# The D term of a state space mixer: products with diagonal matrices on TensorE against a product on VectorE and an add on GpSimd

## The chip, the cores and the metric

The kernel runs on one core of one Trainium2 chip. Its time is the device time of one execution in microseconds (us), taken as the median of three runs. The engines are TensorE (PE in the rows, with its weight loads as PEld), VectorE (DVE), ScalarE (ACT), GpSimd (POOL) and the DMA queues. Each engine works through its own instructions in order; they meet at semaphores.

## The reference, cut to what matters

The model has two layers, and the first begins with a mixer of the Mamba-2 kind over 8 sequences of 512 tokens and 128 features. The scan over time carries a state of 4 heads x 64 x 128; the kernel computes it in chunks of 128 tokens. The D term is the last summand of the line that computes y:

```
xs = silu(conv(x @ in_proj_w.T)[..., :256] + conv_b)        # 256 inner channels, 4 heads of 64
h  = h * dA_t + einsum('bh,bhp,bn->bhpn', dt_t, x_t, B_t)   # for each token
y  = einsum('bhpn,bn->bhp', h, C_t)
y  = ys + D[None, None, :, None] * xs                       # the D term
y  = y * silu(z)
y  = y * rsqrt(mean(y * y) + EPS) * norm_w
out = y @ out_proj_w.T
```

Behind the mixer come a layer of 8 experts, an attention layer and a second layer of experts. The change doesn't touch them.

## The kernel before, in words

The function `mixer` writes one program for each engine. All five step through the same slots s; slot s belongs to sequence b = s // 4 and has the place c = s % 4 in it. In this document "slot c2" is a slot with c = 2. A slot takes up chunk s (128 tokens of 128 partitions), and finishes earlier ones: the product that gives y for chunk t = s - 1, the output projection of chunk s - 2, the norm of chunk s - 3, the logits of chunk s - 4. In the same slot the next sequence (f = b + 1) has a quarter of its convolution computed, and the one after it gets its normalisation. The order within a slot is written out by hand; there is no planner. Sequence 7 has no next one, so in its slots there is no convolution, and from sequence 5 on there are no statistics for a later one.

TensorE in one slot, in order: in slot c3 first a transpose of `da48` (L662), which waits for VectorE's last copy out of bank 7 in the slot before (`o_r`, L569); the transposes of xs and the product B x C of chunk s (L668, L669); the spread of the decays (L675); the transposes of yz, B and xn2 into bank 6 (L683, L685, L689), the first of which waits for yz of chunk s - 2; half of the convolution (three matmuls for each tap, L630 to L632); for chunk t the product with the carried state (L724), then for each half i of the 256 channels one product of the chunk with the diagonal matrix `diag_d[:, i]` (L729) and two products of `mt` with `xdt` that add to the same bank (L732); the new state (L742); the other half of the convolution; the output projection (L755) and the logits (L758).

VectorE in one slot, in order: xdt (L487), the scan that spreads the decays `lt` (L493), y1 = carried part x decay (L499; c = 0 of a sequence has none), mt (L502), in slot c3 the four steps for the next sequence's decays (L507 to L516, the last is da_bd), xn2 (L523; it waits for `rs2` of GpSimd), y2 = y1 + bank 5 (L530), the new state (L535 or, for the first chunk, L538), yz = y2 x silu(z) (L544; for the first chunk L548, straight from the bank), then x (L565; it waits for the output projection), statistics and routing; in slot c2 also ve1 (L586) and h_lo (L610), in slot c3 at its very beginning nm1 (L474).

GpSimd in one slot, in order: state_d = state x decay (L258; chunks with t % 4 of 1 or 2, so slots c2 and c3), in slot c3 the weights wo_g (L265), rs2 (L270, a power of one column), rr (L275, a power of one column, which waits for ScalarE's ysq of this slot), one of the three steps of the residual (L282, L285, L288, in slots c1, c2, c3), and in slot c2 rs1 (L295).

ScalarE evicts the convolution (xc, L397), z (zs, L318) and the transposes, and in slot c1 changes its function table four times; `da` (L388) there waits for VectorE's dax (L598).

At the start GpSimd builds `diag_d` from the identity and the D values, in the loop's slot -7.

Of the kernel before, what the change touches and what calls it, by code (L numbers as in the profile page):

```python
# [10 lines left out]
P = 128  # L11
# [4 lines left out]
ALU = mybir.AluOpType  # L16
# [3 lines left out]
NB = 8  # L20
# [4 lines left out]
DI = 256  # L25
# [82 lines left out]
def mixer(nc, k, a):  # L108
# [5 lines left out]
    with ExitStack() as ctx:  # L114
        def sb(name, shape, dt=F32):
# [2 lines left out]
        wc_hi = sb("wc_hi", [P, NTAP, SEQ], F32R); wc_lo = sb("wc_lo", [P, NTAP, SEQ], F32R)  # L118
        wz = sb("wz", [P, DI + NH]); wz_hi = sb("wz_hi", [P, DI + NH], F32R); wz_lo = sb("wz_lo", [P, DI + NH], F32R)
        conv_b = sb("conv_b", [P, 4]); dt_b = sb("dt_b", [P, NH]); a_log = sb("a_log", [P, NC * NH]); a_exp = sb("a_exp", [P, NC * NH])  # L120
        d_bc = sb("d_bc", [P, DI]); diag_d = sb("diag_d", [P, 2, P]); norm_w = sb("norm_w", [P, 2])
        wo = sb("wo", [P, 2, D]); wo_g = sb("s_wo_g", [P, 2, 2, D]); gw = sb("gw", [P, NE])
        ident4 = sb("ident4", [P, NC * P]); pick = sb("pick", [48, 16]); csel_f = sb("csel_f", [48, NC]); csel = sb("csel", [48, NC], F32R); head = sb("head", [48, NH]); zero16 = sb("zero16", [16, P])
        cT = sb("cT", [P, 2 * NB]); cu = sb("cu", [P, 2 * NB])
# [22 lines left out]

        k.sems((
            "c_in", "c_in1", "x_in0", "x_in1", "x_in2", "w_in0", "w_in1", "w_in2", "aw_in", "pad_in", "r_out") + tuple(f"rows_in{b}" for b in range(NB)) + (
            "set_pool", "set_diag", "set_pick", "c_cu", "c_mm", "c_mod", "c_row_mm", "c_row", "c_gate", "c_rk", "w_mul", "w_hi", "w_lo",  # L150
            "f_mm", "f_ev", "l1_st", "l1_ag", "l1_ve", "l1_rs", "l1_nm", "l1_xn", "h_lo", "res_1", "res_2", "res_x", "s_wog",
            "d_raw", "d_neg", "d_exp", "d_ln", "d_dt", "d_dax", "d_da", "d_hi", "d_t", "d_bd", "o_w", "o_r",
            "s_xmm", "s_lmm", "s_amm", "s_aev", "s_xdt", "s_lt", "s_mt", "s_xdw", "s_ymm", "s_smm", "s_y1", "s_y2", "s_yz", "s_state", "s_sd",
            "s_ss", "s_rr", "o_x", "l2_st", "l2_ag", "l2_ve", "l2_rs", "l2_xn", "r_mx", "r_mi"))
        block = ctx.enter_context(nc.Block())

# [73 lines left out]
        def _(pool):  # L230
# [12 lines left out]
            def body(s, b, c):  # L243
                if s == -7:
                    pool.wait_ge(S["w_in2"], 16 * 6)
                    for i in range(2):
                        ins = g_.tensor_scalar(wo[:, i, :], wo[:, i, :], norm_w[:, i:i + 1], None, ALU.mult)
                    ins.then_inc(S["set_pool"], 1)
                    for i in range(2):
                        ins = g_.tensor_tensor(diag_d[:, i, :], ident[:], d_bc[:, i * P:i * P + P], ALU.mult)  # L250
                    ins.then_inc(S["set_diag"], 1)
                t = s - 1
                if chunk(t) and t % NC in (1, 2):
                    wait(pool, "s_state", n_y(t))
                    wait(pool, "o_r", seventh["cum", t // NC] + 1)
                    wait(pool, "s_state", n_y(t))
                    at = (t % NC) * NH
                    g_.tensor_tensor(hv(state_d[:]), hv(state[:]), bc3(ctot[:, (t // NC) % 2, 1, at:at + NH], NH, HD), ALU.mult).then_inc(S["s_sd"], 1)  # L258
                if b + 1 < NB and c == 3 and b >= -1:
                    f = b + 1  # L260
                    pool.wait_ge(S[f"rows_in{f}"], 16)
                    pool.wait_ge(S["set_pool"], 2)
                    if f >= 2:
                        wait(pool, "o_w", seventh["out", NC * (f - 1) + 1] + 1)
                    g_.tensor_tensor(wo_g[:, f % 2], wo[:], over_rows(rows[:, f, GA0, :], 2), ALU.mult).then_inc(S["s_wog"], 1)  # L265
                t = s - 3
                if chunk(t):
                    wait(pool, "l2_ve", t + 1)
                    wait(pool, "l2_xn", t - 1)
                    g_.tensor_tensor(rs2[:, t % 2, :], ve2[:], half_neg[:, 0:1], ALU.pow).then_inc(S["l2_rs"], 1)  # L270
                t = s - 1
                if chunk(t):
                    wait(pool, "s_ss", t + 1)
                    wait(pool, "o_x", t - 1)
                    g_.tensor_tensor(rr[:, t % 2, :], ss[:, t % 2, :], half_neg[:, 0:1], ALU.pow).then_inc(S["s_rr"], 1)  # L275
                if b >= -1 and b + 1 < NB and c > 0:
                    f = b + 1
                    wait(pool, "l1_xn", f + 1)
                    if c == 1:
                        pool.wait_ge(S[f"rows_in{f}"], 16)  # L280
                        wait(pool, "res_x", f)
                        g_.tensor_tensor(rt[:], xn1[:, f % 2], over_rows(rows[:, f, RES_G, :], NC), ALU.mult).then_inc(S["res_1"], 1)  # L282
                    elif c == 2:
                        wait(pool, "res_1", f + 1)
                        g_.tensor_tensor(rt[:], rt[:], over_rows(rows[:, f, RES_B, :], NC), ALU.add).then_inc(S["res_2"], 1)  # L285
                    else:
                        wait(pool, "res_2", f + 1)
                        g_.tensor_tensor(x[:, f * NC:f * NC + NC, :], x[:, f * NC:f * NC + NC, :], rt[:], ALU.add).then_inc(S["res_x"], 1)  # L288

                g = b + 3  # L290
                if g < NB and c == 2:
                    wait(pool, "l1_ve", g + 1)
                    wait(pool, "l1_nm", g)
                    wait(pool, "l1_xn", g)
                    g_.tensor_tensor(rs1[:], ve1[:], half_neg[:], ALU.pow).then_inc(S["l1_rs"], 1)  # L295
# [121 lines left out]
        def _(dve):  # L417
# [8 lines left out]
            def body(s, b, c):  # L426
# [54 lines left out]
                if chunk(s):  # L481
                    q = b % 2
                    wait(dve, "s_xmm", s + 1)
                    wait(dve, "s_ymm", s - 1)
                    wait(dve, "s_xdw", NH * n_y(s - 1))
                    wait(dve, "d_dt", b + 1)
                    v.tensor_tensor(hv(xdt[:, s % 2, :]), hv(bank[2][:, 0:DI]), bc3(dt[:, q, c * NH:c * NH + NH], NH, HD), ALU.mult).then_inc(S["s_xdt"], 1)  # L487
                if front and c == 1:
                    wait(dve, "d_raw", f + 1)
                    v.scalar_tensor_tensor(out=dtn[:], in0=dtw[:], scalar=-1.0, in1=dtw[:], op0=ALU.mult, op1=ALU.min).then_inc(S["d_neg"], 1)  # L490
# [3 lines left out]
                t = s - 1  # L494
                if chunk(t) and t % NC:
                    wait(dve, "s_ymm", t + 1)
                    wait(dve, "s_y2", n_y(t) - 1)
                    at = (t % NC) * NH
                    v.tensor_tensor(hv(y1[:]), hv(bank[5][:, DI:2 * DI]), bc3(ctot[:, (t // NC) % 2, 0, at:at + NH], NH, HD), ALU.mult).then_inc(S["s_y1"], 1)  # L499
                if chunk(s):  # L500
# [23 lines left out]
                t = s - 1  # L524
                if chunk(t):
                    tb, tc = t // NC, t % NC
                    if tc:
                        wait(dve, "s_y1", n_y(t))
                        wait(dve, "s_yz", t)
                        v.tensor_tensor(y2[:], y1[:], bank[5][:, 0:DI], ALU.add).then_inc(S["s_y2"], 1)  # L530
                    if tc < 3:
                        wait(dve, "s_smm", n_y(t) + 1)
                        if tc:
# [5 lines left out]
                    if t >= 2:  # L539
                        wait(dve, "s_amm", turned[t] + 1)  # L540
                        wait(dve, "s_ss", t - 1)
                    if tc:
                        wait(dve, "s_y2", n_y(t))
                        v.tensor_tensor(yz[:, t % 2, 0:DI], y2[:], zs[:, tb % 2, tc, :], ALU.mult).then_inc(S["s_yz"], 1)  # L544
                    else:
                        wait(dve, "s_ymm", t + 1)
                        wait(dve, "f_ev", ring["z", tb, 3] + 1)
                        v.tensor_tensor(yz[:, t % 2, 0:DI], bank[5][:, 0:DI], zs[:, tb % 2, tc, :], ALU.mult).then_inc(S["s_yz"], 1)  # L548
                if gl < NB and c == 2:
                    wait(dve, "x_in0" if gl == 0 else "x_in1" if gl == 1 else "x_in2", 16)  # L550
                    wait(dve, "l1_ag", NC * gl)
# [68 lines left out]
        def _(pe):  # L620
# [31 lines left out]
            def body(s, b, c):  # L652
# [64 lines left out]
                if chunk(t):  # L717
# [5 lines left out]
                        wait(pe, "s_state", n_y(t))  # L723
                        t_.matmul(bank[5][:, DI:2 * DI], xc[:, tb % 2, 3, tcols], state[:], start=True, stop=True)  # L724
                    if t == 0:
                        pe.wait_ge(S["set_diag"], 1)
                        wait(pe, "c_row", 4)
                    for i in range(2):
                        t_.matmul(bank[5][:, i * P:i * P + P], xc[:, tb % 2, i, tcols], diag_d[:, i, :], start=True, stop=True)  # L729
                        wait(pe, "s_mt", t + 1)  # L730
                        for h in (2 * i, 2 * i + 1):
                            mm = t_.matmul(bank[5][:, h * HD:h * HD + HD], mt[:, t % 2, h * P:h * P + P], xdt[:, t % 2, h * HD:h * HD + HD],  # L732
                                           start=False, stop=True, skip_group_check=True)
                    mm.then_inc(S["s_ymm"], 1)
                    if front and c == 0:
                        z(f, 2)
# [24 lines left out]
            slots(body)  # L761

    k.retired = [(n, NT) for n in (
        "s_xmm", "s_lmm", "s_xdt", "s_lt", "s_mt", "s_ymm", "s_yz", "s_ss", "s_rr", "o_x", "l2_st", "l2_ag", "l2_ve", "l2_rs", "l2_xn", "r_mx", "r_mi",
        "l1_st", "l1_ag")] + [(n, 3 * NB) for n in ("s_smm", "s_y1", "s_y2", "s_state")] + [("s_sd", 2 * NB), ("s_xdw", 3 * NB * NH)] + [(n, NB) for n in (
        "l1_ve", "l1_rs", "l1_nm", "l1_xn", "h_lo", "res_1", "res_2", "res_x", "s_wog", "d_raw", "d_neg", "d_exp", "d_ln", "d_dt", "d_dax", "d_da",
        "d_hi", "d_t", "d_bd")] + [("f_mm", len(ring)), ("f_ev", len(ring)), ("o_w", len(seventh)), ("o_r", len(seventh)), ("s_amm", len(turned)), ("s_aev", len(turned))]

# [917 lines left out]
```

## Time and profile before

| | |
|---|---|
| median of 3 runs | 729.47 us (727.29 to 730.06) |
| profiled execution, own time | 731.17 us |
| its span | 727.9 us |
| mean granted TensorE clock | 0.91 |
| PE busy | 583.6 us (80%) |
| PEld busy | 480.0 us (66%) |
| DVE busy | 427.3 us (59%) |
| ACT busy | 348.9 us (48%) |
| POOL busy | 282.1 us (39%) |

The span runs from the first to the last instruction; the execution's own time is 3.3 us longer. The mixer's loop over chunks takes from about 41 us to about 312 us of the span, the rest belongs to the later layers. Busy shares are means over stages that are bound by different things, so the rows that count for this change are those of the mixer's loop. In a timeline a row can stand for several instructions of one line (x2, x4), and TensorE's instructions overlap, so what one of them takes of the engine is read from start to start.

### The profile page before, as it was taken

What the parts mean: (1) busy time and instruction counts of PE and PEld (TensorE: products, weight loads), DVE (VectorE), ACT (ScalarE), POOL (GpSimd) and SP (SyncE); (2) the same over time, 40 slices, a digit from 0 to 9 for tenths busy, and PEclk for the clock granted to TensorE, in tenths of its full rate; (3) what the DMA queues carried; (4) which work ended last, traced back from release to release, by engine and by line L of the source; (5) the groups of instructions that cost most, each with busy time, mean ns of one, the idle gap of its engine ahead of it and who ended that gap; (6) DMA issues with size and microseconds to landing.
All of it is one profiled execution on the core that took longest, in us unless ns stands there. A gap on an engine that the chain in (4) does not pass through costs nothing.

```text
span 727.9 us, 13867 instructions
## 1 busy us (share of the span) xinstructions
PE 583.6 (80%) x3569; PEld 480.0 (66%) x3569; DVE 427.3 (59%) x1583; ACT 348.9 (48%) x947; POOL 282.1 (39%) x339
## 2 busy tenths in 40 slices
PE   5698989999998998727687787867519999999694
PEld 3577777777777877614465565555519999999631
DVE  4437675758586657843554645355526666666447
ACT  4654748373747453325444434332105666665424
POOL 3303141414232331311104533444545667676423
PEclk9889999999999998958999989899659999999977
DMA  8599999900000000026000000000112222222193
GB/s 272 196 180 176 180 173 179 137 2 1 1 2 1 2 0 1 1 78 193 0 1 24 30 13 19 31 31 30 34 50 60 69 73 67 72 67 73 52 234 101
DMA packets 74846, 52.91 MB, mean 73 GB/s; under 512 B 10392, under 2 KB 68760, under 8 KB 74512
## 3 DMA queue, kind: packets, MB, share of 16 engines
q1 hardware_dynamic: 69200, 41.30, 28.8%
q0 software_dynamic: 4320, 8.99, 3.7%
q10 hardware_dynamic: 1248, 1.71, 0.6%
q8 instruction: 34, 0.56, 0.3%
q14 instruction: 44, 0.36, 0.2%
HBM read 40.88 MB, written 29.48 MB: 97 GB/s over the span
## 4 chain that ended last, share of the span: by engine, by line
PE 37%; DVE 7%; issue 5%; ACT 3%; POOL 1%; DMA 1%; SPq 0%; ACTq 0%; DVEq 0%; POOLq 0%
PE bank L1575 9%; PE bank L1593 9%; PE bank L1492 6%; PE bank L1477 4%; DVE work L1311 1%; PE bank L1468 1%; PE bank L1458 1%; DVE nmx L1294 1%; POOL queue L1066 1%; PE bank L1566 1%; PE bank L1462 1%; ACT work L1166 1%; DVE st_f L1409 1%; ACT h_all L1161 1%; PE bank L1521 1%
## 5 line engine op out<-in xcount | busy, mean ns | idle before, releaser
L1098 POOL DMA_INDIRECT results<-yw,xg x71 | 75.7, 1066 | 56.4 <-ACT yw L1188 51.6
L275 POOL TENSOR_TENSOR rr<-ss,half_neg 128x1 f32<-128x1 f32 x32 | 17.6, 550 | 190.3 <-ACT ysq L403 190.3
L1575 PE MATMUL bank<-xt,wc 128*128 128x128 f32 x568 | 78.0, 281 | 1.2 <-issue 0.7
L1492 PE MATMUL bank<-vv,work 128*128 128x128 f32 x256 | 41.1, 309 | 44.7 <-ACT work L1166 30.0
L1593 PE MATMUL bank<-w,ht 128*128 x568 | 75.8, 277 | 0.1
L1575 PEld LDWEIGHTS bank<-xt,wc 128*128 128x128 f32 x568 | 70.6, 196 | 3.9 <-issue 3.1
L630 PE MATMUL bank<-h_hi,wc_hi 128*128 128x512 f32 x128 | 59.4, 464 | 13.2 <-ACT xc L397 12.2
L1593 PEld LDWEIGHTS bank<-w,ht 128*128 128x128 f32 x568 | 69.7, 193 | 0.3 <-issue 0.3
L1066 POOL DMA_INDIRECT queue<-row,pos x64 | 62.7, 980 | 18.1 <-issue 17.5
L1492 PEld LDWEIGHTS bank<-vv,work 128*128 128x128 f32 x256 | 34.4, 209 | 52.2 <-ACT work L1166 33.5
L1382 DVE COPY wc<-w 128x516 f32 x71 | 36.2, 511 | 37.6 <-PE bank L1575 33.9
L1155 ACT ACTIVATE work<-bank,nmx 128x512 f32<-128x512 f32 x32 | 22.0, 687 | 66.1 <-DVE nmx L1294 66.1
L631 PE MATMUL bank<-h_hi,wc_lo 128*128 128x512 f32 x128 | 52.5, 410 | 0.0
L632 PE MATMUL bank<-h_lo,wc_hi 128*128 128x512 f32 x128 | 52.4, 409 | 0.0
L1395 DVE TENSOR_SCALAR ht<-bank,wc 128x128 f32<-128x128 f32 x142 | 42.8, 342 | 14.0 <-PE bank L1575 13.5
L397 ACT ACTIVATE xc<-bank,conv_b 128x512 f32<-128x512 f32 x32 | 22.0, 687 | 59.4 <-PE bank L632 59.3
L1182 ACT ACTIVATE xt<-bank 128x128 f32<-128x128 f32 x71 | 19.7, 278 | 62.9 <-PE bank L1566 62.4
L1203 ACT ACTIVATE ht<-bank,wc 128x128 f32<-128x128 f32 x142 | 43.2, 353 | 1.4 <-PE bank L1575 1.3
L1075 POOL TENSOR_TENSOR rs_a<-ve_a,half_neg 128x4 f32<-128x4 f32 x8 | 8.2, 1026 | 84.1 <-DVE ve_a L1241 83.1
L630 PEld LDWEIGHTS bank<-h_hi,wc_hi 128*128 128x128 f32 x128 | 25.3, 198 | 21.0 <-ACT xc L397 13.8
L493 DVE TENSOR_TENSOR_SCAN lt<-bank,ident 128x512 f32<-128x512 f32 x32 | 38.8, 1213 | 0.1
L732 PE MATMUL bank<-xdt,mt 128*128 128x64 f32 x256 | 36.5, 266 | 0.0
(276 smaller groups left out, 1491.6 us busy)
## 6 DMA issues: line engine op xcount, KB each, us to landing
queue<-in_pad_rows SPq DMA_DIRECT2D x8, 2178.0 KB, 33.0
xg<-queue SPq DMA_DIRECT2D x71, 66.0 KB, 1.8
w<-in_w SPq DMA_DIRECT2D x2, 2048.0 KB, 10.6
rows<-mod_rows SPq DMA_DIRECT2D x8, 384.0 KB, 5.9
h_all<-results SPq DMA_DIRECT2D x8, 256.0 KB, 4.8
work<-results SPq DMA_DIRECT2D x8, 256.0 KB, 5.4
out_x<-x SPq DMA_DIRECT2D x8, 256.0 KB, 2.3
results<-yw,xg POOLq DMA_INDIRECT x71, 2.4
```

Source lines behind the costliest of these rows:

```text
L493: v.tensor_tensor_scan(lt[:, s % 2, :], bank[3][:], ident4[:], 0.0, ALU.mult, ALU.add).then_inc(S["s_lt"], 1)
L630: t_.matmul(dst, l_hi, r_hi, start=first, stop=False)
L631: t_.matmul(dst, l_lo, r_hi, start=False, stop=False)
L632: return t_.matmul(dst, l_hi, r_lo, start=False, stop=last)
L732: mm = t_.matmul(bank[5][:, h * HD:h * HD + HD], mt[:, t % 2, h * P:h * P + P], xdt[:, t % 2, h * HD:h * HD + HD], start=False, stop=True, ...
L1066: pool.indirect_dma_start(k.queue, bass.IndirectOffsetOnAxis(ap=pos[:, s, i, c:c + 1], axis=0), row[:, s * NC + c, i, :], None).then_inc(S ...
L1098: pool.indirect_dma_start(k.results, bass.IndirectOffsetOnAxis(ap=xg[:, c, D:D + 1].bitcast(I32), axis=0), yw[:, c, :], None).then_inc(S[f ...
L1203: ac.activation(ht[:, p, g * P:g * P + P], bank[2 + p][:, g * P:g * P + P], ACT.Relu, bias=wc[:, p, FF + g:FF + g + 1]).then_inc(S["ht_a"], 1)
L1395: v.tensor_scalar(ht[:, p, g * P:g * P + P], bank[6 + p][:, g * P:g * P + P], wc[:, p, FF + g:FF + g + 1], 0.0, ALU.add, ALU.max).then_inc ...
L1492: mm = t_.matmul(bank[4 if n % 2 else 0][:, 0:D], pt[:, n % 3, i * P:i * P + P], vv[:, s % 2, i, :], start=(i == 0), stop=(i == NC - 1))
L1575: mm = t_.matmul(bank[(2 if g < NG // 2 else 6) + p][:, g * P:g * P + P], wc[:, p, g * P:g * P + P], xt[:, p, :], start=True, stop=True)
L1593: mm = t_.matmul(bank[4 + p][:, 0:D], ht[:, p, g * P:g * P + P], w2[:, e, g, :], start=(g == 0), stop=(g == NG - 1))
```

## The change

The diagonal matrices go. VectorE multiplies the transposed chunk (bank 2) with the D values into a new tile `xd`, right behind xdt. GpSimd adds y1 and xd into a new tile `yx`, as its first step of the slot; VectorE's y2 is then yx plus bank 5. For the first chunk of a sequence, which has no y1, y2 is xd plus bank 5, an instruction that was not there before, and yz always reads y2.

```
-        d_bc = sb("d_bc", [P, DI]); diag_d = sb("diag_d", [P, 2, P]); norm_w = sb("norm_w", [P, 2])
+        d_bc = sb("d_bc", [P, DI]); xd = sb("xd", [P, 2, DI]); yx = sb("yx", [P, DI]); norm_w = sb("norm_w", [P, 2])
...
 @block.gpsimd
-                    for i in range(2):
-                        ins = g_.tensor_tensor(diag_d[:, i, :], ident[:], d_bc[:, i * P:i * P + P], ALU.mult)
-                    ins.then_inc(S["set_diag"], 1)
                 t = s - 1
+                if chunk(t) and t % NC:
+                    wait(pool, "s_y1", n_y(t))
+                    wait(pool, "s_xd", t + 1)
+                    wait(pool, "s_y2", t)
+                    g_.tensor_tensor(yx[:], y1[:], xd[:, t % 2, :], ALU.add).then_inc(S["s_yx"], 1)
                 if chunk(t) and t % NC in (1, 2):
                     wait(pool, "s_state", n_y(t))
...
 @block.vector (behind xdt)
+                if chunk(s):
+                    if s == 0:
+                        dve.wait_ge(S["w_in2"], 16 * 6)
+                    wait(dve, "s_y2", s - 1)
+                    v.tensor_tensor(xd[:, s % 2, :], bank[2][:, 0:DI], d_bc[:], ALU.mult).then_inc(S["s_xd"], 1)
...
                 if chunk(t) and t % NC:
                     wait(dve, "s_ymm", t + 1)
-                    wait(dve, "s_y2", n_y(t) - 1)
+                    wait(dve, "s_yx", n_y(t) - 1)
...
                 if chunk(t):
                     tb, tc = t // NC, t % NC
+                    wait(dve, "s_yz", t)
                     if tc:
-                        wait(dve, "s_y1", n_y(t))
-                        wait(dve, "s_yz", t)
-                        v.tensor_tensor(y2[:], y1[:], bank[5][:, 0:DI], ALU.add).then_inc(S["s_y2"], 1)
+                        wait(dve, "s_yx", n_y(t))
+                    else:
+                        wait(dve, "s_ymm", t + 1)
+                    v.tensor_tensor(y2[:], yx[:] if tc else xd[:, t % 2, :], bank[5][:, 0:DI], ALU.add).then_inc(S["s_y2"], 1)
...
-                    if tc:
-                        wait(dve, "s_y2", n_y(t))
-                        v.tensor_tensor(yz[:, t % 2, 0:DI], y2[:], zs[:, tb % 2, tc, :], ALU.mult).then_inc(S["s_yz"], 1)
-                    else:
-                        wait(dve, "s_ymm", t + 1)
-                        wait(dve, "f_ev", ring["z", tb, 3] + 1)
-                        v.tensor_tensor(yz[:, t % 2, 0:DI], bank[5][:, 0:DI], zs[:, tb % 2, tc, :], ALU.mult).then_inc(S["s_yz"], 1)
+                    wait(dve, "s_y2", t + 1)
+                    wait(dve, "f_ev", ring["z", tb, 3] + 1)
+                    v.tensor_tensor(yz[:, t % 2, 0:DI], y2[:], zs[:, tb % 2, tc, :], ALU.mult).then_inc(S["s_yz"], 1)
...
 @block.tensor
-                    for i in range(2):
-                        t_.matmul(bank[5][:, i * P:i * P + P], xc[:, tb % 2, i, tcols], diag_d[:, i, :], start=True, stop=True)
-                        wait(pe, "s_mt", t + 1)
-                        for h in (2 * i, 2 * i + 1):
-                            mm = t_.matmul(bank[5][:, h * HD:h * HD + HD], mt[:, t % 2, h * P:h * P + P], xdt[:, t % 2, h * HD:h * HD + HD],
-                                           start=False, stop=True, skip_group_check=True)
+                    wait(pe, "s_mt", t + 1)
+                    for h in range(NH):
+                        mm = t_.matmul(bank[5][:, h * HD:h * HD + HD], mt[:, t % 2, h * P:h * P + P], xdt[:, t % 2, h * HD:h * HD + HD], start=True, stop=True)
                     mm.then_inc(S["s_ymm"], 1)
```

## Rows read from the trace of the kernel before

**Rows 1.** Busy time by stretch: length, then each engine's busy us, TensorE's clock, DMA share, GB/s
```profile
140.00:180.00 40.00, 36.49 (x225) 30.37 (x224) 29.22 (x99) 24.56 (x70) 13.15 (x18) 1.00 0.02 4
126.10:129.50 3.40, 3.40 (x12) 2.75 (x11) 0.00 (x0) 2.90 (x9) 2.78 (x4) 0.53 1.25 154
...
283.10:289.90 6.80, 6.70 (x28) 6.04 (x29) 3.77 (x13) 2.33 (x9) 1.10 (x2) 0.51 0.00 1
```

**Rows 2.** One line's instructions: min/median/max ns, first and last start, shapes
```profile
L729 PE MATMUL bank<-diag_d,xc x128: 271/275/527, 51.9 to 302.9; 128*128 128x128 f32 x128
...
L487 DVE TENSOR_TENSOR xdt<-bank,dt x32: 403/424/426, 42.0 to 297.5; 128x256 f32<-128x256 f32 x32
```

**Rows 3.** Who waited for whom, 50 to 310 us: us in total, times, longest
```profile
DVE y L499 <- PE bank L732: 43.0, 22, 5.5
DVE x L565 <- PE bank L758: 23.7, 15, 2.3
...
ACT da L388 <- DVE dax L598: 5.4, 6, 1.1
```

**Rows 4.** Timeline of TensorE, slots c2 and c3 of sequence 3: start, us
```profile
163.05 0.38 PE L729 MATMUL bank<-diag_d,xc 128*128 128x128 f32 x2
163.27 0.56 PE L732 MATMUL bank<-xdt,mt 128*128 128x64 f32 x4
163.66 0.44 PE L729 MATMUL bank<-diag_d,xc 128*128 128x128 f32 x2
163.94 0.56 PE L732 MATMUL bank<-xdt,mt 128*128 128x64 f32 x4
...
167.97 0.29 PE L662 MATMUL bank<-ident,da 128*48 128x128 f32 x1 [1.02 <-DVE lg L569]
...
176.86 0.41 PE L683 MATMUL bank<-ident,yz 128*128 128x128 f32 x2 [0.39 <-DVE yz L544]
```

**Rows 5.** Timeline of VectorE over the same two slots
```profile
164.53 0.42 DVE L499 TENSOR_TENSOR y<-bank,ctot 128x256 f32<-128x256 f32 x1 [3.89 <-PE bank L732]
...
165.47 0.34 DVE L523 TENSOR_SCALAR xn<-x,mv,rs 128x128 f32<-128x128 f32 x1
...
168.29 1.08 DVE L586 TENSOR_SCALAR ve<-mv 128x4 f32<-128x4 f32 x1
...
170.52 0.57 DVE L474 SCALAR_TENSOR_TENSOR nm<-mv,rs 128x4 f32<-128x4 f32 x1
...
172.77 0.42 DVE L499 TENSOR_TENSOR y<-bank,ctot 128x256 f32<-128x256 f32 x1 [0.22 <-PE bank L732]
...
174.65 0.68 DVE L516 TENSOR_TENSOR da_bd<-da,head 48x512 fp32r<-48x512 f32 x1
175.26 0.33 DVE L523 TENSOR_SCALAR xn<-x,mv,rs 128x128 f32<-128x128 f32 x1
```

**Rows 6.** Timeline of GpSimd over the same two slots
```profile
168.09 1.27 POOL L285 TENSOR_TENSOR rt<-rt,rows 128x512 f32<-128x512 f32 x1
...
170.45 0.62 POOL L258 TENSOR_TENSOR state_d<-state,ctot 128x256 f32<-128x256 f32 x1
171.02 0.73 POOL L265 TENSOR_TENSOR s_wo_g<-wo,rows 128x256 f32<-128x256 f32 x1
171.71 0.54 POOL L270 TENSOR_TENSOR rs<-ve,half_neg 128x1 f32<-128x1 f32 x1
```

**Rows 7.** Timeline of GpSimd, slot c2 of sequence 5
```profile
235.96 1.75 POOL L285 TENSOR_TENSOR rt<-rt,rows 128x512 f32<-128x512 f32 x1
```

**Rows 8.** Timeline of VectorE, slot c2 of sequence 6
```profile
265.72 0.35 DVE L523 TENSOR_SCALAR xn<-x,mv,rs 128x128 f32<-128x128 f32 x1 [0.97 <-POOL rs L270]
```

**Rows 9.** Timeline of TensorE: the beginning of slot c2's convolution, sequences 2 and 3
```profile
125.59 0.57 PE L630 MATMUL bank<-h_hi,wc_hi 128*128 128x512 f32 x1 [1.39 <-ACT xc L397]
...
161.12 0.50 PE L630 MATMUL bank<-h_hi,wc_hi 128*128 128x512 f32 x1 [1.38 <-ACT xc L397]
```

**Rows 10.** Timeline of VectorE, the last three y1, of sequence 7
```profile
294.15 0.42 DVE L499 TENSOR_TENSOR y<-bank,ctot 128x256 f32<-128x256 f32 x1 [0.41 <-PE bank L732]
...
298.97 0.40 DVE L499 TENSOR_TENSOR y<-bank,ctot 128x256 f32<-128x256 f32 x1
...
303.63 0.42 DVE L499 TENSOR_TENSOR y<-bank,ctot 128x256 f32<-128x256 f32 x1 [1.28 <-PE bank L732]
```

More of the change, by code:

```diff
@@ L149, in mixer @@
             "c_in", "c_in1", "x_in0", "x_in1", "x_in2", "w_in0", "w_in1", "w_in2", "aw_in", "pad_in", "r_out") + tuple(f"rows_in{b}" for b in range(NB)) + (
-            "set_pool", "set_diag", "set_pick", "c_cu", "c_mm", "c_mod", "c_row_mm", "c_row", "c_gate", "c_rk", "w_mul", "w_hi", "w_lo",
+            "set_pool", "set_pick", "c_cu", "c_mm", "c_mod", "c_row_mm", "c_row", "c_gate", "c_rk", "w_mul", "w_hi", "w_lo",
             "f_mm", "f_ev", "l1_st", "l1_ag", "l1_ve", "l1_rs", "l1_nm", "l1_xn", "h_lo", "res_1", "res_2", "res_x", "s_wog",
             "d_raw", "d_neg", "d_exp", "d_ln", "d_dt", "d_dax", "d_da", "d_hi", "d_t", "d_bd", "o_w", "o_r",
-            "s_xmm", "s_lmm", "s_amm", "s_aev", "s_xdt", "s_lt", "s_mt", "s_xdw", "s_ymm", "s_smm", "s_y1", "s_y2", "s_yz", "s_state", "s_sd",
+            "s_xmm", "s_lmm", "s_amm", "s_aev", "s_xdt", "s_lt", "s_mt", "s_xdw", "s_ymm", "s_smm", "s_y1", "s_xd", "s_yx", "s_y2", "s_yz", "s_state", "s_sd",
             "s_ss", "s_rr", "o_x", "l2_st", "l2_ag", "l2_ve", "l2_rs", "l2_xn", "r_mx", "r_mi"))
@@ L725, in body @@
                     if t == 0:
-                        pe.wait_ge(S["set_diag"], 1)
                         wait(pe, "c_row", 4)
-                    for i in range(2):
-                        t_.matmul(bank[5][:, i * P:i * P + P], xc[:, tb % 2, i, tcols], diag_d[:, i, :], start=True, stop=True)
-                        wait(pe, "s_mt", t + 1)
-                        for h in (2 * i, 2 * i + 1):
-                            mm = t_.matmul(bank[5][:, h * HD:h * HD + HD], mt[:, t % 2, h * P:h * P + P], xdt[:, t % 2, h * HD:h * HD + HD],
-                                           start=False, stop=True, skip_group_check=True)
+                    wait(pe, "s_mt", t + 1)
+                    for h in range(NH):
+                        mm = t_.matmul(bank[5][:, h * HD:h * HD + HD], mt[:, t % 2, h * P:h * P + P], xdt[:, t % 2, h * HD:h * HD + HD], start=True, stop=True)
                     mm.then_inc(S["s_ymm"], 1)
@@ L763, in mixer @@
     k.retired = [(n, NT) for n in (
-        "s_xmm", "s_lmm", "s_xdt", "s_lt", "s_mt", "s_ymm", "s_yz", "s_ss", "s_rr", "o_x", "l2_st", "l2_ag", "l2_ve", "l2_rs", "l2_xn", "r_mx", "r_mi",
-        "l1_st", "l1_ag")] + [(n, 3 * NB) for n in ("s_smm", "s_y1", "s_y2", "s_state")] + [("s_sd", 2 * NB), ("s_xdw", 3 * NB * NH)] + [(n, NB) for n in (
+        "s_xmm", "s_lmm", "s_xdt", "s_lt", "s_mt", "s_ymm", "s_xd", "s_y2", "s_yz", "s_ss", "s_rr", "o_x", "l2_st", "l2_ag", "l2_ve", "l2_rs", "l2_xn", "r_mx", "r_mi",
+        "l1_st", "l1_ag")] + [(n, 3 * NB) for n in ("s_smm", "s_y1", "s_yx", "s_state")] + [("s_sd", 2 * NB), ("s_xdw", 3 * NB * NH)] + [(n, NB) for n in (
         "l1_ve", "l1_rs", "l1_nm", "l1_xn", "h_lo", "res_1", "res_2", "res_x", "s_wog", "d_raw", "d_neg", "d_exp", "d_ln", "d_dt", "d_dax", "d_da",
```

## The prediction

> **What bounds the kernel now.** I began with the busy time by stretch. In 40 us in the middle of the mixer's loop TensorE is busy for 36.49 us at full clock, VectorE for 29.22 [rows 1]. So TensorE looks like the bound, and work taken from it like time won. The table of waits says the same from the other side: VectorE stood 43.0 us before y1 for the product L732, and 23.7 us before x for the projection [rows 3]. But TensorE is idle for 3.5 us of these 40, and the timelines tell where, once in every sequence. It waits 1.38 us in slot c2 for ScalarE's xc [rows 9], 1.02 us at the head of slot c3 for VectorE's last copy, and 0.39 us at the head of slot c0 for yz [rows 4]. Between the last two, VectorE has work from y1 at 164.53 to yz at the end of slot c3 with gaps of a tenth or two only: it waits for nothing but 0.22 us before y1 of slot c3 [rows 5]. So the path round one sequence (33.9 us) is TensorE from the head of c0 to L732 in c2, with a leg over ScalarE, and then VectorE from y1 in c2 to yz in c3. Work taken from TensorE in the first part shortens the path, work or waits put on VectorE in the second lengthen it.
>
> **What it removes from TensorE.** L729 is there 128 times [rows 2], two passes for each of two products in each of 32 chunks. From start to start a pair takes 163.27 - 163.05 = 0.22 us and 163.94 - 163.66 = 0.28 us [rows 4], so 0.50 us a chunk, 16 us in all if every chunk were on the path. In a sequence three of four are (c0, c1, c2): -1.5 us. For c1 the leg over ScalarE must follow: its da waits for VectorE's dax, 5.4 us in 6 sequences [rows 3], 0.9 us each. The 1.0 us saved up to there just about fits; I count it whole.
>
> **What it adds to VectorE.** xd is a product of a bank and a tile, as xdt is, 0.42 us long [rows 2], 0.34 us from start to start in the stretches that are packed. The additional y2 of a sequence's first chunk costs as much, up to 0.55 with the wait of yz behind it. In c0 and c1 both hide in VectorE's wait for the projection (23.7 us in 15 times, so 1.6 us each [rows 3]); in c2 xd hides in the 3.89 us before y1 [rows 5]. In c3 xd is on the path; if its cover were gone in c0 and c1 as well, it would cost 0.7 us more a sequence.
>
> **What it adds to GpSimd, and what stands behind it.** yx waits for y1, and GpSimd works in order. Behind it stand state_d, in c3 wo_g, and rs2; VectorE's xn2 waits for rs2, and xn2 stands ahead of y2, the state and yz. Until now these were done long before y1 (in c3 rs2 began at 171.71 [rows 6], y1 at 172.77 [rows 5]). yx itself is in no row. The nearest is state_d, of the same size, 0.62 us and 0.57 to the next one's start [rows 6]; the ends are 0.54 (the smallest instruction, rs2) and 0.73 (wo_g). I take 0.57 a step. In c2: y1 ends at 164.95, then 0.07 for the semaphore, yx 0.57, state_d 0.57, rs2 0.55, 0.04 back: xn2 starts at 166.75 and not at 165.47 [rows 5], +1.28 us (+1.2 to +1.5 by those ends). That VectorE does stop there when rs2 is late is seen once already, with 0.97 us [rows 8]. In c3 wo_g adds 0.69: xn2 is 2.49 us behind the end of y1, before it was 175.26 - 173.19 = 2.07 [rows 5]: +0.42.
>
> The ve1 and nm1 rows show one more thing. ve1, four columns, takes 1.08 us and ends at 169.37, with GpSimd's 512-wide L285, at 169.36; nm1, four columns, takes 0.57 and ends at 171.09, with state_d, at 171.07 [rows 5, 6]. So some instructions of VectorE wait until GpSimd's has ended. And L285 took 1.75 us, not 1.27, when it started into h_lo [rows 6, 7]. In c3 da_bd (two tiles of SBUF, 174.65) now meets wo_g and rs2. It can be held for about 0.5 us and can hold rs2 for as long: between nothing and +0.5 us, I take +0.23. The other way, state_d is no longer in front of nm1, since yx now stands in between and waits: nm1 falls to about 0.15, -0.41 us. The Trainium skill ("GPSIMD Engine Reference", Key points) says that GpSimd shares its SBUF interfaces with VectorE and contends with VectorE instructions that have two SBUF inputs or a 2-port mode; the trace agrees (1.08 us for four columns). The same page (Engine selection) says to keep two-input elementwise work on VectorE, as GpSimd is about 2x slower. Here it is 0.62 to 0.42, 1.5x; by the page's factor yx would take 0.84, and the sum would be some 3 us higher.
>
> The build of the diagonals at the start, two small instructions of GpSimd, is worth nothing: at most 1.2 us of an engine that has nothing else to do there.
>
> **The sum.** Sequences 1 to 4, each: -1.5 (TensorE), +1.28 (c2), then in c3 up to y1 -0.41 (nm1), +0.34 (xd), -0.22 (the wait before y1 goes, TensorE being 0.5 earlier) and -0.1 (ve1 ends with an L285 that begins a little earlier), together -0.4, and +0.65 before yz: +0.03 each (-0.3 to +0.5), so +0.1. Sequence 0 gains nothing in c0 and c1 and has no xn2 in c2 yet: +0.25. Sequences 5 and 6 have no nm1, but VectorE waits before y1 of c3, so TensorE's fourth 0.5 counts too: -0.3 each. Sequence 7 has no convolution and so no cover. Its VectorE has hardly a wait left from 294.15 on (0.41, none, 1.28 before the three y1 [rows 10]). In its c0 +0.5 (xn2 behind rs2), in c1 -1.0 (TensorE at half clock there [rows 1], so 2 x 0.5), in c2 -0.1 and +1.28, in c3 +0.34 (xd) and +1.28, in the slot after it -0.5 and +1.3: +3.1. Together about +2.7 us.
>
> **The clock.** In two stretches of 3.4 us inside the full loop the granted clock was at the lower level, 1.2 GHz instead of 2.4: from 126.1 us (0.53 [rows 1]) and again from 269.5. The first came right after TensorE had waited 1.39 us [rows 9]. The same wait of 1.38 at 161.12 brought none [rows 9]: after waits of this length a fall can come or stay away. In the new kernel TensorE is done 1.5 us earlier in c2 and released 0.2 us earlier at the head of c3: its wait grows from 1.02 to about 2.3 us in each of sequences 1 to 4 (5 and 6: 1.5 to 2.4). Longer waits make it likelier, I take it, and what follows this one, up to L732 of c3, has less than 0.2 us of slack. One fall costs at most 3.4 x 0.47 = 1.6 us. I count three to four more falls at 1.2: +4.3 us, with 0 and 6 x 1.6 = 9.6 as ends.
>
> Against the profiled execution: 731.17 + 2.7 + 4.3 = 738.2 us. Its own time lies 1.7 above the median of the runs, 729.47, so the forecast for the median is 736.5 us.
>
> **The rivals.**
> 1. The stall without the clock: waits of 2.3 us bring no more falls than before. For it: four of five waits like those in rows 9 passed unpunished. Only +2.7 is left: 732.2 us, within 0.5%.
> 2. TensorE's saving arrives (the other side). The mechanism is in c2 and c3: if xn2 didn't have to stand behind rs2, -1.5 to -2.0 a sequence would stay over. It decides at the point where GpSimd's chain behind y1 is shorter than VectorE's cover in front of xn2 (0.52 us in c2 [rows 5]). 8 x -1.9 = -15, so 714 us; with half of the stalls gone, 722. Against it: the order is fixed, and 0.57 a step is measured.
> 3. Collisions of GpSimd and VectorE cost more than I take: yx, state_d and rs2 now all run while VectorE works on mt, state and da_bd, and each can be stretched by 0.5 us as in rows 7. Two such in each sequence: +8, with my sum 744 us, or 740 without more falls.
>
> **How the numbers follow.** Forecast with falls 0.50 (733.5 to 740); rival 1: 0.23; rival 2: 0.12; rival 3: 0.15. A measurement of this kernel tells 0.5% (3.6 us) from no change. Faster than 725.8: 0.12. Within: rival 1 and the lowest part of the forecast, 0.24. Slower than 733.1: 0.64. The range leaves out most of rival 2 and the upper part of rival 3: 728 to 743; the forecast's own is 733 to 740.
>
> **What would show it right or wrong.** TensorE without L729, and L732 0.5 us earlier behind the convolution. In slots c2 an idle of about 1.2 us before xn2 (L523 before) put down to GpSimd's rs2, in c3 about 0.3. nm1 at 0.15 us. TensorE's wait at the head of c3 at 2.3 us instead of 1.02, and more low stretches of the granted clock. Three stalls of 1.3 us in sequence 7. The period of a sequence 33.9 us without a fall, 35 with one. It is wrong if xn2 has no such wait, if periods are 32 us, or if the wait at c3 stays near 1 us.

## The result, and the profile after

The changed kernel takes 762.05 us (757.76 to 765.18, 4 runs) where the kernel before takes 729.76 (727.29 to 730.13, 4 runs). The ratio is 1.0446, 95% interval 1.0386 to 1.0506: slower by 32 us. The direction was forecast, the size was not: 736.5 us, range 728 to 743. Medians are of all executions of a kernel, ratios only of those that nothing slowed down as a whole; where the two differ, the ratio is the figure to go by.

The profiled execution took 760.48 us, with a span of 757.8 and a mean granted clock of 0.872 (before 0.910). The page's first part, then its rows for TensorE and its clock:

```profile
PE 592.7 (78%) x3441; PEld 487.9 (64%) x3441; DVE 442.4 (58%) x1623; ACT 349.7 (46%) x947; POOL 301.7 (40%) x361
...
PE   4797979797879898772677777777536999999874
...
PEclk9789799989997989555799999999856999999988
```

128 instructions of TensorE are gone, and TensorE is busy for 9 us longer, 592.7 after 583.6. Less work takes more time: what is left of it runs at the lower clock for longer. The busy time by stretch shows where (columns as in [rows 1]): the second row is the mixer's loop from 60 us to its end, the first a stretch inside it.

```profile
228.90:239.00 10.10, 9.76 (x36) 8.48 (x37) 5.34 (x18) 5.23 (x20) 3.03 (x4) 0.53 0.01 2
60.00:353.10 293.10, 244.03 (x1224) 203.33 (x1222) 191.53 (x634) 138.57 (x384) 99.95 (x137) 0.83 0.35 50
```

The loop ends at 353.1 us; before it ended at 315.3, with a mean clock of 0.96 from 60 us on. A mean of 0.83 over 293.1 us is 293.1 x 0.17 x 2 = 100 us at the lower level, 1.2 GHz; before it was 255.3 x 0.04 x 2 = 20 us. About 30 us of the difference lie behind the head of sequence 7. The other 50 lie in the sequences before, and there each low stretch begins with a wait at the head of c3 or of c0, or less than 2 us behind it. TensorE's waits and what follows them (timeline, sequences 4 and 5; before in [rows 4]):

```profile
210.37 0.50 PE L635 MATMUL bank<-h_hi,wc_hi 128*128 128x512 f32 x1 [1.39 <-ACT xc L399]
...
218.22 0.29 PE L667 MATMUL bank<-ident,da 128*48 128x128 f32 x1 [2.45 <-DVE lg L574]
...
221.29 0.63 PE L635 MATMUL bank<-h_hi,wc_hi 128*128 128x512 f32 x1
...
229.24 0.41 PE L688 MATMUL bank<-ident,yz 128*128 128x128 f32 x2 [1.42 <-DVE yz L553]
```

The wait at the head of c3 grew from 1.02 to 2.45 us, as forecast (2.3). The one for yz at the head of c0 grew from 0.39 to 1.42, which the prediction did not look at. In the rows shown the clock falls behind both: a product of 128x512 takes 0.63 us and not 0.40, and behind 229.24 the clock stays low for 10 us (0.53 in the first stretch above), through the transposes, z and the small products of slot c0. The periods of a sequence, from one copy of the state to the next, are 37.8, 37.6, 39.0, 36.5, 40.5, 36.7 and 36.0 us; before they were 32.5, 33.9, 35.5, 33.9, 33.9, 33.4 and 33.2.

The rest of the program, which the change doesn't touch, took 404.7 us in this execution and 412.6 in the one before. It had fewer low stretches there (some 80 us at the lower level and not 99), so that of the 37.8 us more in the mixer 29.9 are left in the span. In the traces of the other kernels this part takes 403 to 412 us, so a trace's span says less about the mixer than the time at which its loop ends.

What VectorE and GpSimd do in those slots (timelines, sequence 4, slots c2 and c3):

```profile
213.35 0.42 DVE L506 TENSOR_TENSOR y<-bank,ctot 128x256 f32<-128x256 f32 x1 [3.12 <-PE bank L734]
...
215.71 0.35 DVE L530 TENSOR_SCALAR xn<-x,mv,rs 128x128 f32<-128x128 f32 x1 [1.34 <-POOL rs L272]
...
220.62 0.17 DVE L476 SCALAR_TENSOR_TENSOR nm<-mv,rs 128x4 f32<-128x4 f32 x1
...
224.14 0.42 DVE L506 TENSOR_TENSOR y<-bank,ctot 128x256 f32<-128x256 f32 x1 [1.46 <-PE bank L734]
...
226.02 1.16 DVE L523 TENSOR_TENSOR da_bd<-da,head 48x512 fp32r<-48x512 f32 x1
227.63 0.35 DVE L530 TENSOR_SCALAR xn<-x,mv,rs 128x128 f32<-128x128 f32 x1 [0.45 <-POOL rs L272]
```
```profile
213.86 0.74 POOL L254 TENSOR_TENSOR yx<-y,xd 128x256 f32<-128x256 f32 x1 [1.27 <-DVE y L506]
214.56 0.61 POOL L260 TENSOR_TENSOR state_d<-state,ctot 128x256 f32<-128x256 f32 x1
215.13 0.55 POOL L272 TENSOR_TENSOR rs<-ve,half_neg 128x1 f32<-128x1 f32 x1
...
225.91 0.73 POOL L267 TENSOR_TENSOR s_wo_g<-wo,rows 128x256 f32<-128x256 f32 x1
226.60 1.00 POOL L272 TENSOR_TENSOR rs<-ve,half_neg 128x1 f32<-128x1 f32 x1
```

xn2 stands behind rs2 for 1.34 us, nm1 is down to 0.17 (0.57 in [rows 5]), da_bd is up from 0.68 to 1.16 and holds rs2, 1.00 instead of 0.54 [rows 6]. Each of these steps was forecast. At 224.14 VectorE waits 1.46 us for the slow products of TensorE: there the clock comes onto the path.

### The profile page after: what moved, and what is told of

It is laid out like the page before. It is cut to its first block, busy times and chain, and to the rows that moved or that the text cites. A ratio compares the mean times of both kernels' runs of the same rounds, so it can differ in the third digit from the quotient of the medians.

```text
span 757.8 us, 13728 instructions
## 1 busy us (share of the span) xinstructions
PE 592.7 (78%) x3441; PEld 487.9 (64%) x3441; DVE 442.4 (58%) x1623; ACT 349.7 (46%) x947; POOL 301.7 (40%) x361
## 3 DMA queue, kind: packets, MB, share of 16 engines
q10 hardware_dynamic: 1248, 1.71, 0.6%
## 4 chain that ended last, share of the span: by engine, by line
PE 34%; DVE 7%; issue 5%; ACT 3%; POOL 1%; DMA 1%; SPq 0%; ACTq 0%; DVEq 0%; POOLq 0%
PE bank L1576 9%; PE bank L1594 8%; PE bank L1493 5%; PE bank L1478 4%; DVE work L1312 1%; DVE nmx L1295 1%; PE bank L1459 1%; POOL queue L1067 1%; PE bank L1469 1%; PE bank L1567 1%; ACT work L1167 1%; PE bank L1463 1%; DVE st_f L1410 1%; ACT h_all L1162 1%; PE bank L1522 1%
## 5 line engine op out<-in xcount | busy, mean ns | idle before, releaser
L1493 PE MATMUL bank<-vv,work 128*128 128x128 f32 x256 | 39.3, 299 | 44.4 <-ACT work L1167 29.6
L635 PE MATMUL bank<-h_hi,wc_hi 128*128 128x512 f32 x128 | 63.5, 496 | 13.3 <-ACT xc L399 12.7
L636 PE MATMUL bank<-h_hi,wc_lo 128*128 128x512 f32 x128 | 56.1, 438 | 0.0
L637 PE MATMUL bank<-h_lo,wc_hi 128*128 128x512 f32 x128 | 55.1, 431 | 0.0
L734 PEld LDWEIGHTS bank<-xdt,mt 128*128 128x128 f32 x256 | 42.9, 238 | 3.3
L254 POOL TENSOR_TENSOR yx<-y,xd 128x256 f32<-128x256 f32 x24 | 17.7, 739 | 65.5 <-DVE y L506 65.5
L635 PEld LDWEIGHTS bank<-h_hi,wc_hi 128*128 128x128 f32 x128 | 27.5, 215 | 21.8 <-ACT xc L399 14.3
L734 PE MATMUL bank<-xdt,mt 128*128 128x64 f32 x256 | 40.1, 312 | 0.0
```

Source lines behind the costliest of these rows:

```text
L635: t_.matmul(dst, l_hi, r_hi, start=first, stop=False)
L636: t_.matmul(dst, l_lo, r_hi, start=False, stop=False)
L637: return t_.matmul(dst, l_hi, r_lo, start=False, stop=last)
L1493: mm = t_.matmul(bank[4 if n % 2 else 0][:, 0:D], pt[:, n % 3, i * P:i * P + P], vv[:, s % 2, i, :], start=(i == 0), stop=(i == NC - 1))
```

## The experiments

Theory A: the path by waits is nearly as long as before, and the rest is the clock, brought down by the longer waits that GpSimd's order makes. Rivals: B, the waits are the time and the clock only goes with them; C, the clock falls because TensorE has less to do; D, the cause is xd on VectorE. Four kernels ran side by side (the kernel before: 728.3 us).

**GpSimd's order.** yx moved behind rs2:

```
-                if chunk(t) and t % NC: ... yx ...        # first step of the slot
                 ... state_d, wo_g, rs2 ...
+                if chunk(t) and t % NC: ... yx ...        # behind rs2, ahead of rr
```

> The changed kernel with one thing moved: GpSimd does yx after state_d, wo_g and rs2 instead of ahead of them, so xn2 and the state no longer stand behind it; y2 alone still waits for it. Theory A (the longer path starts GpSimd's order behind y1, and the longer waits of TensorE bring the clock down): per sequence -1.5 us on TensorE, y2 at most 0.1 later, xn2 without a wait: 720 to 728 us, with the waits at the heads of slots c3 and c0 back at about 1.0 and 0.4 to 0.9 us and a mean clock of 0.90 or more. Rival C (what brings the clock down is the work taken from TensorE, whatever GpSimd does): the clock stays near 0.87 and the time is 735 to 750. Rival D (xd on VectorE is the cause): 755 or more.

Measured: 719.21 us, ratio 0.9888 (0.9835 to 0.9941). The same instructions on every engine, in another order on one, and 43 us less. TensorE's wait at the head of c3 and GpSimd in front of it:

```profile
162.55 0.29 PE L667 MATMUL bank<-ident,da 128*48 128x128 f32 x1 [1.20 <-DVE lg L574]
```
```profile
159.45 0.75 POOL L273 TENSOR_TENSOR yx<-y,xd 128x256 f32<-128x256 f32 x1 [0.18 <-DVE y L506]
```

xn2 (L530) no longer waits for rs2 in sequences 1 to 5, the clock is at full level from 60 to 220 us, and a sequence takes 31.7 to 33.0 us. C and D fall as explanations of the 32 us: the lighter TensorE and xd are both there. It came in just under the range A gave it.

**The D term left out.** What the removed work is worth:

```
-                        t_.matmul(bank[5][:, i * P:i * P + P], xc[:, tb % 2, i, tcols], diag_d[:, i, :], start=True, stop=True)
...
-                                           start=False, stop=True, skip_group_check=True)
+                        ... start=True, stop=True)
```

> The kernel before with the products with the diagonal matrices left out and nothing in their place (the D term is missing from the result). It shows what the removed work of TensorE is worth by itself, and whether the granted clock stands the lighter load. Theory A: three of four chunks on the path, -1.5 us a sequence and some in the last one: 716 to 721 us, clock 0.90 or more. Rival C (the lighter load brings the clock down by itself): 727 or more, clock below 0.89. If TensorE were the bound everywhere: 714.

Measured: 713.26 us, ratio 0.9812 (0.9757 to 0.9867); seven periods of 31.6 to 32.3 us, mean clock 0.914. That is below A's range, and as a time it is what the bound "TensorE everywhere" gave, 714. The periods decide between the two: 1.6 us of 33.9 came off in a sequence without a fall, the 1.5 counted for three chunks and not the 2.0 of four. The rest of the 15 us isn't the mixer's path. In the profiled execution the mixer ends at 306.2 us, 9.1 earlier than before, and the other 8.6 us of the shorter span lie in the part that the edit doesn't touch.

The last sequence shows a small part of C. Up to 256 us the clock is at full level in the loop, but behind that it is low for some 32 us (about 20 before), and from the last copy of the state to the loop's end it takes 28.8 us where it took 24.9. This kernel differs from the one before by the lighter TensorE alone.

**An add on GpSimd alone.** The kernel before, D term on TensorE, with

```
                 t = s - 1
+                if chunk(t) and t % NC:
+                    wait(pool, "s_y1", n_y(t))
+                    g_.tensor_tensor(yx[:], y1[:], d_bc[:], ALU.add).then_inc(S["s_yx"], 1)
                 if chunk(t) and t % NC in (1, 2):
```

and y1's wait for it, so that it doesn't overwrite what is being read.

> The kernel before with one instruction added: GpSimd adds y1 and a constant tile as its first step of the slot, as yx stands in the changed kernel; nobody uses the result, the D term stays on TensorE. Theory A: xn2 waits for rs2 by 1.3 us in slots c2, about 0.5 to 0.9 in c3 with da_bd at 1.16 us, nm1 down to 0.17: +2 us a sequence by the path alone (745), more with the clock's falls behind the longer waits: 750 to 762 us, clock 0.88 or less. Rival C (the lighter TensorE load is needed for the falls): 742 to 748 and a clock of 0.90 or more. Rival D (xd is the cause): 730.

Measured: 762.43 us, ratio 1.0405 (1.0327 to 1.0482), by which it is about 758 us. One unused instruction of 0.74 us, 24 times, costs 30 us. The same waits stand in its timelines as in the changed kernel's, VectorE first, TensorE second:

```profile
175.78 0.35 DVE L527 TENSOR_SCALAR xn<-x,mv,rs 128x128 f32<-128x128 f32 x1 [1.34 <-POOL rs L273]
...
187.90 1.16 DVE L520 TENSOR_TENSOR da_bd<-da,head 48x512 fp32r<-48x512 f32 x1
```
```profile
178.29 0.41 PE L666 MATMUL bank<-ident,da 128*48 128x128 f32 x1 [2.45 <-DVE lg L573]
...
191.11 0.41 PE L687 MATMUL bank<-ident,yz 128*128 128x128 f32 x2 [1.38 <-DVE yz L548]
```

The time is in A's range, the clock is not: its two quickest executions have a mean of 0.90, which is what C had, where A had 0.88 or less and the changed kernel has 0.87. The loop in this trace (60 to 352.2 us, clock 0.89; the profiled execution took 766.4 us) has 64 us at the lower level, between the 20 before and the 100 of the changed kernel. Three of its periods take 37.9 us with one low stretch of 3.4 us each. By the prediction's price of at most 1.6 us for such a fall, 36.3 us or more are path: 2.4 us more than before, where A had 2. So the falls need neither xd nor a lighter TensorE, but this kernel's 30 us are path and clock in about equal parts (an estimate: 7 x 2.4 = 17 us of path), while in the changed kernel the 32 are mostly clock (29, below). No two kernels with these waits differ by the lighter TensorE alone, so what it adds to the falls stays open.

**The waits filled.** The changed kernel, with products that nobody reads in TensorE's two long waits:

```
+                def fill(i, n):
+                    for _ in range(n):
+                        t_.matmul(bank[i][:], wc_hi[:, 0, 0:P], wc_hi[:, 1, :], start=True, stop=True)
+                if chunk(s) and c == 3:
+                    wait(pe, "s_mt", s)
+                    wait(pe, "s_xdt", s)
+                    fill(2, 9)
...
+                        if c == 0:
+                            fill(6, 5)
                         wait(pe, "s_yz", t + 1)
```

> The changed kernel with work put into TensorE's two long waits: ahead of the one at the head of slot c3 nine products 128x512 (some 2.1 us) into bank 2, ahead of the one for yz at the head of slot c0 five (some 1.2 us) into bank 6, all overwritten afterwards. The path by waits is unchanged or slightly longer. Theory A (most of the 32 us is the granted clock): mean clock 0.91 or more in the loop, 736 to 744 us. Rival B (the waits themselves are the time, the clock only goes with them): 758 to 766 us, whatever the clock does.

Measured: 732.49 us (10 runs), ratio 1.0043 (1.0008 to 1.0078). More work on TensorE, and 30 us less. The loop from 60 to 300 us, the filled wait in c3, and two copies of the state, one sequence apart, with xn2 between them:

```profile
60.00:300.00 240.00, 226.22 (x1272) 184.42 (x1271) 176.67 (x574) 132.43 (x369) 93.90 (x126) 0.99 0.43 61
```
```profile
201.84 2.33 PE L665 MATMUL bank<-wc_hi 128*128 128x512 f32 x9
...
204.43 0.29 PE L676 MATMUL bank<-ident,da 128*48 128x128 f32 x1 [0.26 <-DVE lg L574]
```
```profile
191.57 0.42 DVE L547 COPY state<-bank 128x256 f32<-128x256 f32 x1
...
201.93 0.35 DVE L530 TENSOR_SCALAR xn<-x,mv,rs 128x128 f32<-128x128 f32 x1 [1.35 <-POOL rs L272]
...
226.10 0.42 DVE L547 COPY state<-bank 128x256 f32<-128x256 f32 x1
```

The clock is at 0.99, and VectorE's stall of 1.35 us in c2 is still there: the path by waits is that of the changed kernel. It takes 34.5 us a sequence; before it was 33.9. That refutes B, and it measures the clock's part: 29 of the 32 us. The traces agree: the loop ends at 323.8 us, 29.3 earlier than in the changed kernel, with 21 us at the lower level (263.8 us at 0.96) and not 100. It came in below A's range.

What is left for the path is 3 us by the ratio. By the traces it is more: the loop ends 8.5 us later than before, with about the same time at the lower level, and 6.5 of these lie behind the last copy of the state (31.4 us to the loop's end, before 24.9), where fillers stand too. The rest of the program was 3.1 us shorter in that execution. So the path's part is 3 to 8 us.

**Which wait.** The same fillers at one place only, the other left open:

> The changed kernel with only the wait at the head of slot c3 filled (nine products 128x512 into bank 2); the wait for yz at the head of slot c0 stays 1.4 us long. With both filled the time was 732.5 us, with none 762. Theory A1 (the falls begin in the longest wait, the 2.45 us at c3): 735 to 742. Theory A2 (the falls behind the wait at c0 last longer, since the transposes, z and the small products come next, and cost more): 742 to 752, with low stretches left behind the head of c0.

Measured: 743.96 us, ratio 1.0208 (1.0155 to 1.0261); clock 0.93 from 60 to 300 us:

```profile
60.00:300.00 240.00, 216.66 (x1175) 178.60 (x1173) 167.94 (x550) 127.96 (x351) 90.30 (x122) 0.93 0.47 62
```

> The changed kernel with only the wait for yz at the head of slot c0 filled (five products into bank 6); the 2.45 us at the head of c3 stay. Theory A1: 752 to 760, since a low stretch of 3.4 us stays behind the head of c3 in nearly every sequence. Theory A2: 738 to 746.

Measured: 740.37 us, ratio 1.0143 (1.0079 to 1.0206); clock 0.95:

```profile
60.00:300.00 240.00, 212.07 (x1167) 173.22 (x1166) 171.08 (x555) 130.06 (x361) 91.69 (x123) 0.95 0.43 61
```

Both lie in the ranges of A2 and outside A1's, the first by 2 us. Left open alone, the shorter wait, 1.4 us before c0, costs 11 us over the 732.5 of both filled, the one of 2.45 us before c3 costs 8. The traces show what A2 says: with c0 open the clock falls behind its head in sequences 1 to 4 and stays low for 3.4, 6.8, 7.0 and 6.8 us, with c3 open five stretches of 3.4 us are left between 90 and 220 us, three of them behind the head of c3 and two behind the wait for ScalarE's xc. The two savings, 18 and 22 us, are more than the 30 of both together, so the two waits don't act independently; by what way isn't shown.

**The price of xd, and rs2 ahead of state_d.** Two more beside them (the kernel before: 728.6 us):

> The kernel before without the D term (713.3 us), and with the product xd on VectorE in every chunk, used by nobody. The price of xd by itself. By the path it counts in slot c3 only, 0.34 less the 0.22 of the wait before y1: +1 to +3 us, 714 to 716. If VectorE's waits in c0 and c1 don't cover it: 0.34 in every chunk, 724. The rest up to 719.2 is then y2's wait for GpSimd.

Measured: 716.27 us, ratio 0.9840 (0.9786 to 0.9894), 3 us above the kernel without D term (whose run was on another occasion). That is the upper end of what was expected; the intervals of the two ratios overlap.

> yx behind rs2 as in the first experiment, and besides rs2 ahead of state_d, so that in slot c3 GpSimd does a power of one column and not state_d while VectorE does nm1. If nm1 (0.57 us) is held by state_d and it is on the path, it falls to 0.17 and 0.4 us come back in each of five sequences: 717 us where yx behind rs2 alone gave 719.2. If nm1 is not on the path: 719.

The edit moves rs2 to the top of GpSimd's slot. Measured: 715.32 us, ratio 0.9808 (0.9748 to 0.9868). nm1 before this move and after it:

```profile
164.96 0.57 DVE L476 SCALAR_TENSOR_TENSOR nm<-mv,rs 128x4 f32<-128x4 f32 x1
```
```profile
163.79 0.16 DVE L476 SCALAR_TENSOR_TENSOR nm<-mv,rs 128x4 f32<-128x4 f32 x1
```

The trace shows the mechanism, and the periods of the first five sequences are 0.3 us shorter each than with yx behind rs2 alone. The 4 us of gain are more than the 2 it accounts for, and the intervals of the two ratios (0.9888 and 0.9808) overlap.

**The last sequence.** The same kernel again, and with its last sequence filled (bank 0, nine products ahead of the projection in c0, five ahead of each wait for yz from c2 on), five rounds:

> The same kernel as in the run with rs2 ahead of state_d, measured again in five rounds beside its variant with the filled tail: 715 us, ratio to the kernel before 0.981.

Measured: 718.22 us, ratio 0.9897 (0.9837 to 0.9957), beside 725.5 for the kernel before on this occasion. The first value, 0.981, was lucky; the intervals overlap, and both say faster than the kernel before. Against yx behind rs2 alone (0.9888) no gain in time is shown.

> The kernel with yx behind rs2 and rs2 ahead of state_d, and in the last sequence, where no convolution keeps TensorE busy, products 128x512 into the free bank 0 ahead of its waits: nine ahead of the projection in c0, five ahead of each wait for yz from slot c2 on. The last 40 us of the mixer run at the lower clock now. If the clock is what those slots wait for, 3 to 5 us come back: 711 us. If VectorE bounds them alone: 715, or a little more where a filler is in the way.

Measured: 710.99 us, ratio 0.9813 (0.9758 to 0.9867), 7 us below its twin in the same rounds. The mixer's end from 260 us on, without the fillers (trace of the first run with rs2 ahead of state_d) and with them:

```profile
260.00:308.60 48.60, 34.36 (x171) 28.93 (x169) 33.70 (x121) 13.26 (x44) 13.92 (x23) 0.71 0.00 1
```
```profile
260.00:302.20 42.20, 32.98 (x194) 26.74 (x192) 33.33 (x120) 12.77 (x42) 13.12 (x21) 0.90 0.00 1
```

So the fastest version has the change, yx behind rs2 and rs2 first, and the fillers: 711 us on an occasion where the kernel before took 725.5. About half of these 14.5 us is the fillers' part, and whether fillers would help the kernel before as well was not run.

## Why the prediction was right in direction and wrong in size

- What bounds the kernel: right. The path from TensorE in c0 to c2 and then over VectorE was confirmed by the periods of the kernel without D term: 1.6 us a sequence came off, where the path said 1.5 and TensorE as the bound in all four chunks 2.0. Its 15 us in all look like the latter's 16, but the trace has only 9 of them in the mixer.
- GpSimd's chain before xn2: right. Forecast +1.28 us in c2, measured a wait of 1.34. yx takes 0.74 us with 0.70 to the next start, 1.8 times VectorE's 0.42 for the same size; I took 0.57 from state_d, and wo_g with 0.73 was the closer row.
- The collision in c3: right in kind, at its upper end. da_bd 0.68 to 1.16 and rs2 0.54 to 1.00, of which I took half. nm1's gain of 0.41 was there.
- The sum of the path: +0.03 us a sequence forecast, -0.3 to +0.5 as bounds; +0.6 measured with the waits filled (34.5 us after 33.9), just outside them. For the kernel +2.7 forecast (its own terms add up to 2.85), +3.1 (ratio 1.0043) measured. That closeness is in part luck: in the profiled executions it is +8.5 in the mixer, 6.5 of it behind the last copy of the state, where the sum had +3.1 for all of sequence 7.
- The failed step is the term "the clock": +4.3 us, at most 9.6; measured 29. Four things in it were wrong. It looked for falls only behind the wait at the head of c3; L683's wait of 0.39 us for yz stood in my rows, it grew to 1.42, and the run with c3 filled shows that with this wait left open the time stays at 744. It took each fall as 3.4 us at the lower level; behind the head of c0 the clock stays there for up to 10 us. It capped the number at six, where the loop now has some 80 us more at that level. And it counted nothing for sequence 7, where some 30 of these 80 us lie.
- Rival 1 (stalls without falls, 732.2 us) is what the kernel does when its waits are filled: 732.5. Rival 2 (the saving arrives if xn2 needn't stand behind rs2) is what it does with yx behind rs2: I gave 714 us for that, 719 and with rs2 first 715 and 718 were measured.

## What to carry to other kernels

Before an instruction with a wait is put into an engine's queue, write down what stands behind it there and who waits for that. Here the order of four instructions on an engine that is 40% busy made the difference between +32 and -9 us. And where TensorE is the bound at full clock, price a wait that lengthens by the clock behind it, at every place where TensorE waits and not at the longest only; here products that nobody reads, put into the two waits, gave back 30 of the 32 us.

## What the runs showed of the hardware

Waits of 1.4 us, once in some 35 us of otherwise busy time, can bring TensorE's clock to its lower level, and one of 1.4 us before the head of c0 cost at least as much as one of 2.45 us before the head of c3 (11 and 8 us, each left open alone): in the changed kernel the clock was granted at 0.53 for 10 us behind the former, although TensorE was busy for 9.76 of these 10.1 us; what it did there first were transposes, z and the other small products of slot c0. Behind other waits at the head of c0 it stayed low for 3.4 to 7 us, and once (193.04 us, 1.71 us of waiting) it didn't fall. Waits of 1.39 us for ScalarE in c2, ahead of dense convolution, are in all these kernels and mostly brought no fall (none of five in the changed kernel, one of five in the kernel before). Why the one kind has the longer falls is not settled by these runs.

Instructions of VectorE and GpSimd hold each other up in both directions: da_bd with two tiles of SBUF goes from 0.68 to 1.16 us beside GpSimd's wo_g, and a power of one column on GpSimd from 0.54 to 1.00 beside da_bd. VectorE's nm1, four columns, takes 0.57 us beside state_d and 0.16 when the order on GpSimd is changed.
